# Cross attention on one core: K and V of a block, and Q, projected on the whole TensorE array in one place instead of in 64x64 quarters

## The reference

```python
Q = (x @ W_Q)      # 16 heads of 64 columns
K = (ctx @ W_K)
V = (ctx @ W_V)
scores = einsum('bhqd,bhkd->bhqk', Q, K) / sqrt(64)
attn = softmax(scores, axis=-1)
context = einsum('bhqk,bhkd->bhqd', attn, V)   # heads side by side again
out = context @ W_O + x
return (out - mean(out)) / sqrt(var(out) + 1e-05)
```

## Time and profile before

| | |
|---|---|
| median of 3 runs | 1628.64 us (1628.42 to 1628.89) |
| profiled execution | 1629.81 us |
| span in its trace | 1627.9 us |
| mean granted TensorE clock | 0.997 of full speed |
| TensorE matmuls busy | 1612.7 us (99%), 17422 instructions |
| TensorE weight loads busy | 643.8 us (40%) |
| VectorE busy | 1210.3 us (74%) |
| ScalarE busy | 955.5 us (59%) |
| GpSimd busy | 58.8 us (4%) |

### The profile page before, as it was taken

How to read it: one execution, slowest core, us unless ns; L and a number is a source line. 1 busy time by engine, 2 the same in 40 slices (tenths; PEclk the granted TensorE clock), 3 DMA queues, 4 the chain that set the end, 5 groups by cost and what they waited for, 6 DMA issues and landing times.

```text
span 1627.9 us, 39517 instructions
## 1 busy us (share of the span) xinstructions
PE 1612.7 (99%) x17422; PEld 643.8 (40%) x17422; DVE 1210.3 (74%) x1214; ACT 955.5 (59%) x1064; POOL 58.8 (4%) x38
## 2 busy tenths in 40 slices
PE   9999999999999999999999999999999999999997
PEld 3443344333443334433344333443344433444334
DVE  5778787787877778777787777778777787777876
ACT  5556565655556656565655656555665565655652
POOL 0000000000000000000000000000000000000100
PEclk9999999999999999999999999999999999999998
DMA  4000000000000000000000000000000000000000
GB/s 159 2 2 8 2 8 2 1 8 2 8 2 2 8 1 9 2 1 9 1 9 2 2 8 2 9 2 2 8 1 9 2 8 2 2 9 2 8 2 14
DMA packets 12366, 13.76 MB, mean 8 GB/s; under 512 B 4512, under 2 KB 8096, under 8 KB 12192
## 3 DMA queue, kind: packets, MB, share of 16 engines
q1 hardware_dynamic: 11760, 10.61, 2.0%
q10 hardware_dynamic: 432, 0.59, 0.1%
HBM read 10.36 MB, written 0.59 MB: 7 GB/s over the span
## 4 chain that ended last, share of the span: by engine, by line
PE 98%; DVE 1%; DMA 0%; ACT 0%; issue 0%; SPq 0%; ACTq 0%
PE o_ps L374 43%; PE s_ps L357 43%; PE w_ps L421 6%; PE w_ps L404 5%; PE s_ps L444 0%; DMA ctx_all<-in_ctxT 0%; PE o_ps L444 0%; PE w_ps L444 0%; ACT probs L538 0%; DVE sums L637 0%; DVE k_all L625 0%; DVE y L731 0%; DVE limits L741 0%; DVE y L714 0%; PE o_ps L421 0%
## 5 line engine op out<-in xcount | busy, mean ns | idle before, releaser
L637 DVE TENSOR_TENSOR sums<-sums,probs 128x1024 f32<-128x1024 f32 (+1 forms) x800 | 997.6, 1247 | 376.4 <-ACT probs L538 372.3
L538 ACT ACTIVATE probs<-s_ps 128x1024 f32<-128x1024 f32 x816 | 834.9, 1023 | 639.5 <-PE s_ps L357 621.4
L357 PE MATMUL s_ps<-q_sb,k_all 64*64 64x512 f32 x6528 | 847.9, 589 | 0.8 <-DVE q_sb L625 0.6
L374 PE MATMUL o_ps<-probs,v_all 64*64 64x512 f32 x6528 | 847.7, 589 | 0.0
L357 PEld LDWEIGHTS s_ps<-q_sb,k_all 64*64 64x64 f32 x6528 | 251.1, 133 | 449.9 <-issue 447.0
L374 PEld LDWEIGHTS o_ps<-probs,v_all 64*64 64x64 f32 x6528 | 246.8, 133 | 390.8 <-issue 385.5
L404 PEld LDWEIGHTS w_ps<-wv_sb,ctx_all 64*64 64x64 f32 x3232 | 97.2, 133 | 57.6 <-issue 51.8
L421 PE MATMUL w_ps<-ctx_all,wk_sb 64*64 64x512 f32 (+1 forms) x832 | 107.1, 585 | 0.5 <-DMA ctx_all<-in_ctxT 0.5
L404 PE MATMUL w_ps<-wv_sb,ctx_all 64*64 64x128 f32 x3232 | 106.9, 269 | 0.4 <-DVE k_all L625 0.4
L625 DVE TENSOR_TENSOR k_all<-k_all,w_ps 128x512 f32<-128x512 f32 (+1 forms) x104 | 69.6, 670 | 6.8 <-ACT k_all L546 6.8
L332 POOL TENSOR_TENSOR o_b<-o_a,o_b 128x512 f32<-128x512 f32 x15 | 31.5, 2097 | 1116.2 <-ACT o_a L568 1116.2
(11 more groups left out here) (59 smaller groups left out, 104.8 us busy)
## 6 DMA issues: line engine op xcount, KB each, us to landing
inv_sum<-inv_dram SPq DMA_DIRECT2D x30, 128.0 KB, 2.8
ctx_all<-in_ctxT SPq DMA_DIRECT2D x12, 256.0 KB, 5.6
quad_rows<-quad_sums SPq DMA_DIRECT2D x60, 4.0 KB, 1.7
xT_sb<-in_xT ACTq DMA_DIRECT2D x2, 256.0 KB, 4.6
x_sb<-in_x SPq DMA_DIRECT2D x1, 512.0 KB, 10.1
wo_sb<-in_wo SPq DMA_DIRECT2D x1, 512.0 KB, 11.1
out<-y SPq DMA_DIRECT2D x4, 128.0 KB, 1.8
wq_sb<-in_wq SPq DMA_DIRECT2D x1, 448.0 KB, 6.9
```

What stands on the lines that cost most here:

```text
L357: last = nc.tensor.matmul(s_ps[part(half), u % 2, head * QH:(head + 1) * QH], k_all[part(head), c * P + half * DH:c * P + (half + 1) * DH] ...
L374: last = nc.tensor.matmul(o_ps[part(head), rows, :], v_all[part(rows), c, part(head)], probs[part(rows), u % RING, head * QH:(head + 1) * QH],
L538: nc.scalar.activation(probs[:, u % RING, :], s_ps[:, u % 2, :], ACT.Exp, scale=SCALE).then_inc(probs_ready, 1)
L637: nc.vector.tensor_tensor(out=sums[0:rows, t % 2, :], in0=sums[0:rows, t % 2, :], in1=probs[0:rows, u % RING, :], op=ALU.add).then_inc(sum ...
```

## The change

The pieces "k" and "v" of a block become one piece "x" at K's old place (103 of them), for all blocks but the first three pieces. Its K is one matmul with all 128 rows and all 128 columns of the array, into the first bank; its V is one 128x128 matmul for each chunk of 128 keys, into the second bank. Q, but for its first piece, is one 128x128 matmul into the first bank (15 pieces). No sum is split any more. ScalarE copies the first bank (K or Q), VectorE the second (V), side by side; VectorE raises `work_ready` once both are done, and for Q does nothing else. Scores and products are as before, in quarters. TensorE now waits, ahead of the first pair's pieces, for the first columns of all three weights.

```diff
         if h == 0:
-            if t == 0 and c in (0, 1, 7):
-                return {0: ("k", 0, 1), 1: ("v", 0, 1), 7: ("q", 0, 1)}[c]
+            if t == 0 and c in (0, 7):
+                return {0: ("x", 0, 1), 7: ("q", 0, 1)}[c]
             at = c - 2 if t == 0 else c
             if at >= 0 and at % 4 == 0 and at // 4 + 2 < BLOCKS:
-                return ("k", pair, at // 4 + 2)
-            if at >= 2 and at % 4 == 2 and at // 4 + 2 < BLOCKS:
-                return ("v", pair, at // 4 + 2)
-        elif pair + 1 < PAIRS and c in (0, 36, 38, 40, 42, 44):
-            n = (0, 36, 38, 40, 42, 44).index(c)
-            return (("q", "q", "k", "v", "k", "v")[n], pair + 1, (0, 1, 0, 0, 1, 1)[n])
+                return ("x", pair, at // 4 + 2)
+        elif pair + 1 < PAIRS and c in (0, 36, 38, 42):
+            n = (0, 36, 38, 42).index(c)
+            return (("q", "q", "x", "x")[n], pair + 1, (0, 1, 0, 1)[n])
...
+    def k_count(pair, b):
+        return COUNT["k" if (pair, b) == (0, 0) else "x", pair, b]
+
+    def v_count(pair, b):
+        return COUNT["v" if (pair, b) == (0, 0) else "x", pair, b]
...
                 if c % BLOCK == 0 and h == 0:
-                    pe.wait_ge(work_ready, COUNT["k", pair, c // BLOCK])
+                    pe.wait_ge(work_ready, k_count(pair, c // BLOCK))
...
                 if c % BLOCK == 0 and t % 2 == 0:
-                    pe.wait_ge(work_ready, COUNT["v", t // 2, c // BLOCK])
+                    pe.wait_ge(work_ready, v_count(t // 2, c // BLOCK))
...
+                if kind in "xq" and found not in FIRST:
+                    if at == 0:
+                        for first in first_w_loaded.values():
+                            pe.wait_ge(first, 16)
+                    else:
+                        pe.wait_ge(rest_w_loaded, 48)
+                    if kind == "q":
+                        if at == 0:
+                            pe.wait_ge(x_loaded[b], 16)
+                        nc.tensor.matmul(banks[0][:, :], wq_sb[:, at * P:(at + 1) * P], xT_sb[:, b * QH:(b + 1) * QH],
+                                         start=True, stop=True).then_inc(work_done, 1)
+                        return
+                    if at == 0:
+                        pe.wait_ge(ctx_loaded[b], 16)
+                    nc.tensor.matmul(banks[0][:, 0:cols_in(b)], wk_sb[:, at * P:(at + 1) * P],
+                                     ctx_all[:, b * BK:b * BK + cols_in(b)], start=True, stop=True)
+                    for m in range(cols_in(b) // P):
+                        at_key = b * BK + m * P
+                        last = nc.tensor.matmul(banks[1][:, m * P:(m + 1) * P], ctx_all[:, at_key:at_key + P],
+                                                wv_sb[:, at * P:(at + 1) * P], start=True, stop=True)
+                    last.then_inc(work_done, 1)
+                    return
...
             def add_half(found):
                 target, n = target_of(found)
+                if found[0] == "x":
+                    dve.wait_ge(work_done, COUNT[found])
+                    values, n = target_of(("v",) + found[1:])
+                    nc.vector.tensor_copy(values, banks_of(found)[1][:, 0:n]).then_inc(v_taken, 1)
+                    dve.wait_ge(v_taken, 1 + [f for f in COUNT if f[0] == "x"].index(found))
+                    dve.wait_ge(work_half, COUNT[found])
+                    dve.sem_inc(work_ready, 1)
+                    return
+                if found[0] == "q" and found not in FIRST:
+                    dve.wait_ge(work_half, COUNT[found])
+                    dve.sem_inc(work_ready, 1)
+                    return
```

More of the change, by code:

```diff
@@ L153, in cross_attention_kernel @@
         work_ready = sem("work_ready")
+        v_taken = sem("v_taken")
         scores_ready = sem("scores_ready")
@@ L219, in target_of @@
             kind, at, b = found
-            if kind == "k":
+            if kind in "kx":
                 return k_all[:, b * BK:b * BK + cols_in(b)], cols_in(b)
```

## The result

The changed kernel takes 1671.46 us in the median of 4 runs (1671.12 to 1671.79), against 1628.77 (4 runs) for the kernel before, run beside it: 42.7 us more, a ratio of 1.0261 with a 95% interval of 1.0247 to 1.0275. The forecast was 1671, with +42.5. The interval is some 2 us wide to either side, so the last tenths of that agreement mean nothing. The span of the profiled execution is 1669.9 us; its execution took 1671.79. Copying from PSUM with one operation for each sum made VectorE and ScalarE freer, and the kernel is 2.6% slower all the same.

The account below looks back on a forecast made before the run. TensorE's array input was taken to bound the kernel. Passages +41.3, V +2.1, K and Q +0.5 and first-pass stalls -1.4 made +42.5 us, so 1671 us; range 1650 to 1690.

Parts of the forecast that it names:

- The bound: Whole kernel: limited by how long TensorE's array input is occupied; all waiting of TensorE in the loop about 2.9 us.
- Array time of the sums: K, V, Q matmuls: whole-array work buys no array time; V +2.1 us, K and Q +0.5 us.
- Entering: Passage from 64x64 to 128x128 at each K and V or Q place: drain and load wait, 0.21 us.
- the rival: At the 118 places: changing shape is free, the earlier delay came from semaphore waits; +1.2 us, 1630; chance 0.08.
- Leaving: Passage from 128x128 back to 64x64 at each place: 0.14 us, with bounds 0 and 0.29.
- only entering costs: At the 118 places: small loads begin once the last big matmul is fed; +26 us, 1655; chance 0.11.
- the empty pipeline at 0.66: At each place TensorE's whole pipeline empties both ways, 0.66 us; +79 us, 1708; chance 0.14, with more than 0.5 a place.
- The count: 103 K and V places and 15 of Q: 118 at 0.35 us each, +41.3 us.
- The signs of being right: Steady timeline: first whole-array load near T+0.95 for scores at T, scores to product about 0.86 + 2.1 us.
- The first pass: First pass: V's and Q's waits for K's add, 0.62 and 0.69 us too long, go: -1.4 us.
- Off the path: Evictions: some 60 us less for ScalarE and 80 us less for VectorE, both already idle, so no time gained there.

Follow-up runs that it names:

- run in quarters: Changed kernel's places, waits and copies, but K, V and Q streamed as 64x64 matmuls, sums of halves left out: 1627.62 us, ratio 0.9991.

## Why the prediction was right, point by point

**The bound.** TensorE's input was full in the kernel before, and every other engine had room. The run in quarters and the run with both copies on ScalarE show that only array time counts here.

**Array time of the sums.** Forecast 0.862 for K and 0.894 for V. K to V is 203.68 - 202.72 = 0.96, less 0.10 of waiting for the load: 0.86, which fits the forecast and 0.858 alike, so the +0.5 us for K and Q can't be told from nothing. V's eight matmuls last 1.05 from the first start to the last end, and the last is 0.275 long: (1.05 - 0.275)/7 = 0.111 apart, or 0.89 for eight, as forecast. Whole-array matmuls buy no array time, and cost next to none.

**Entering.** Forecast 0.21, from a single passage behind the last pass. Scores to K is 0.97 for 0.86, which is 0.11 of drain (0.02 of it is the spread between the tiles of the last round, 1.04 - 0.589 - 0.429), and 0.10 of load: 0.21. The semaphore waits that the rival blamed had no part: the run in quarters has every wait of the changed kernel and none of the cost.

**Leaving.** This was the term with no row, bounded by 0 and 0.29 and taken as 0.14. The next load begins 0.98 behind the first V matmul. Seven spacings of 0.112 and 0.107 of stream make 0.89, which leaves 0.09 of drain. The product then takes 0.91 for 0.86, 0.05 for its loads. Together that is 0.14. The forecast had put this number together from the drain of the entry and a restart behind a wait, neither of which showed a passage in this direction: the step was a good guess between wide bounds, and the trace bore it out. The case "only entering costs" is out, and so is the empty pipeline at 0.66.

**The count.** Counted from the timeline and not from the times: scores at 201.75 to scores at 205.57 is 3.82 us, where four groups in quarters take 3 x 0.858 + 0.873 = 3.45, so a K and V place costs 0.37. 103 x 0.37 + 15 x 0.36 - 1.4 makes 42, so the places account for the whole loss of 42.7 us (42.0 between the two profiled executions). The signs of being right are there too: the first whole-array load comes at T+0.96 for a forecast T+0.95.

**The first pass.** Both stalls of the earlier trace rows are gone. The timeline of the changed kernel there:

```profile
26.97 1.12 PE L405 MATMUL w_ps<-ctx_all,wk_sb 128*128 128x512 f32 x2
...
28.92 1.09 PE L380 MATMUL o_ps<-probs,v_all 64*64 64x512 f32 x8
29.83 1.04 PE L363 MATMUL s_ps<-q_sb,k_all 64*64 64x512 f32 x8
30.79 1.13 PE L400 MATMUL w_ps<-xT_sb,wq_sb 128*128 128x512 f32 x2
```

Q starts 0.97 behind its scores (29.83 to 30.79), the passage alone, and not a wait for V's copy. The 1.4 us fit the run in quarters, whose interval is wider than the effect, so they rest on the traces: 0.62 and 0.69 of waiting that stood in the earlier trace rows and no longer stand.

**Off the path, one size was off.** I had said 60 us less for ScalarE and 80 for VectorE; their busy time fell by 36 and 70. The copies that went had partly lain over their neighbours, so that an operation taken away saved less busy time than its length. Before, V's copy began at 204.20, when the exponential begun at 203.28 still had 0.10 to run; the copy that stays stands by itself, 0.81 behind the exponential (ScalarE's timeline of the kernel before, then of the changed one):

```profile
204.20 0.59 ACT L546 ACTIVATE v_all<-w_ps 128x512 f32<-128x512 f32 x1
```

```profile
204.77 0.60 ACT L574 ACTIVATE k_all<-w_ps 128x512 f32<-128x512 f32 x1 [0.81 <-PE w_ps L409]
```

It changes no time.

## What to carry to other kernels

When TensorE's input is full, count first what a change does to the stream of matmuls: fewer, larger instructions and freer copy engines gained nothing here. A stretch of work in another shape than its surroundings cost one passage in and one out, 0.36 us here for 128x128 among 64x64 and 0.30 for 128x64. It was nearly the same with one K, one Q or K and V together inside, and more, 0.47, with a single column, whose stream hides no load. So make such stretches few and long, or keep the surrounding shape and pay the split sum on idle engines. A single passage in the trace of before, at its end, was enough to price the way in; the way out had to be guessed from it, with bounds of 0 and 0.29. Only passages from 64x64 and back, with 32-bit data at a granted clock of 1.00, were measured.

## What the runs showed that was not expected

A matmul of one column in one quarter, of the same shape as its surroundings, cost 0.114 us at each of 103 places (1640.83 against 1629.08 us), over twice the most I had allowed. A very short matmul in a full stream wasn't free here even without a change of shape.
